# First attention: one ones-column product per unit on a VectorE sum, for units of three and four key blocks

## The reference

```python
qg = q.reshape(b, HKV, G, s, D)
scores = jnp.einsum('bkgqd,bkpd->bkgqp', qg, k) * scale
scores = jnp.where(causal, scores, jnp.float32(-1e+30))
probs = jax.nn.softmax(scores, axis=-1)
out = jnp.einsum('bkgqp,bkpd->bkgqd', probs, v).reshape(b, H, s, D)
```

## Time and profile before

| what | value |
|---|---|
| runs | 1920.54, 1912.13, 1920.51 us |
| median | 1920.51 us |
| span of the profiled execution | 1921.2 us, 0.7 us above the median |
| TensorE busy | 1731.9 us, 90% |
| VectorE busy | 1151.9 us, 60% |
| ScalarE, GpSimd busy | 708.0 us (37%), 784.0 us (41%) |
| granted TensorE clock, mean | 0.980 of full speed; 1.00 in the stretches up to 800 us |
| last column maxima of a 3-block unit of the first attention | at 770.3 us |
| window 130 to 770 us | TensorE 613.39, VectorE 439.00, GpSimd 347.89, ScalarE 254.90 of 640 us |

### The profile page before, as it was taken

How to read it: one execution, slowest core, us unless ns; L and a number is a source line. 1 busy time by engine, 2 the same in 40 slices (tenths; PEclk the granted TensorE clock), 3 DMA queues, 4 the chain that set the end, 5 groups by cost and what they waited for, 6 DMA issues and landing times.

```text
span 1921.2 us, 76644 instructions
## 1 busy us (share of the span) xinstructions
PE 1731.9 (90%) x34928; PEld 1286.5 (67%) x34928; DVE 1151.9 (60%) x2281; ACT 708.0 (37%) x1073; POOL 784.0 (41%) x760
## 2 busy tenths in 40 slices
PE   6899999999999999798999989899899898878993
PEld 4667777777777767564562767677676676668883
DVE  4656666666787875667337655666666566544324
ACT  2333444344334333342430333343333343334341
POOL 2555646564646463324250403325232343015442
PEclk9999999999999999998999999999999999989997
DMA  9600000000000000300021123131321313025666
GB/s 306 203 2 2 2 2 2 2 2 2 2 2 2 2 2 2 111 1 1 1 67 19 40 61 77 40 87 46 84 73 43 85 44 84 20 66 179 205 205 185
DMA packets 81043, 113.48 MB, mean 59 GB/s; under 512 B 9485, under 2 KB 63505, under 8 KB 80288
## 3 DMA queue, kind: packets, MB, share of 16 engines
q1 hardware_dynamic: 71376, 97.16, 18.6%
q0 software_dynamic: 4544, 8.54, 1.3%
q10 hardware_dynamic: 4800, 2.89, 0.6%
HBM read 83.25 MB, written 45.68 MB: 67 GB/s over the span
## 4 chain that ended last, share of the span: by engine, by line
PE 66%; DVE 18%; issue 5%; ACT 4%; DMA 4%; POOL 2%; POOLq 0%; ACTq 0%; SPq 0%; DVEq 0%
PE psum L1189 63%; DVE colmax L1935 3%; DMA arena<-in_pack 3%; ACT prob L1664 3%; DVE colmax L2092 2%; DVE ctx_sum L1947 2%; DVE raw L1923 1%; DVE rowmax L1942 1%; PE psum L1544 1%; DVE arena L2028 1%; DVE rowmax L2100 1%; PE psum L1256 1%; ACT arena L1681 1%; PE psum L1264 1%; DVE prob L1987 1%
## 5 line engine op out<-in xcount | busy, mean ns | idle before, releaser
L1189 PE MATMUL psum<-arena 128*32 128x32 f32 (+8 forms) x10552 | 576.8, 247 | 43.9 <-issue 17.2
L1189 PEld LDWEIGHTS psum<-arena 128*32 128x32 f32 (+4 forms) x10552 | 453.5, 124 | 135.1 <-issue 61.0
L1681 ACT ACTIVATE arena<-psum 128x1024 f32<-128x1024 f32 (+1 forms) x192 | 169.4, 882 | 339.8 <-PE psum L1189 339.8
L1189 PE MATMUL psum<-neg_ident,rowmax 128*32 128x128 bf16 (+3 forms) x4352 | 208.2, 248 | 10.1 <-issue 8.4
L1935 DVE TENSOR_REDUCE colmax<-psum 128x512 bf16<-128x2048 f32 (+2 forms) x96 | 168.3, 1753 | 79.4 <-PE psum L1189 79.4
L2092 DVE TENSOR_REDUCE colmax<-psum 128x256 bf16<-128x768 f32 (+2 forms) x160 | 178.2, 1114 | 59.7 <-PE psum L1189 57.3
L1189 PE MATMUL psum<-prob,ffw 128*32 128x128 f32 x5120 | 201.5, 275 | 10.9 <-DVE rowmax L1942 9.6
L1696 ACT COPY ctx_sum<-psum 128x384 f32<-128x384 f32 x128 | 61.4, 479 | 378.4 <-PE psum L1189 330.8
L2330 POOL TENSOR_TENSOR arena<-ctx_sum 128x256 f32<-128x256 f32 x128 | 94.7, 740 | 228.5 <-DVE ctx_sum L1947 216.9
L2100 DVE TENSOR_REDUCE rowmax<-psum 128x2 bf16<-128x256 f32 (+1 forms) x192 | 97.9, 510 | 145.8 <-PE psum L1189 145.7
L1664 ACT ACTIVATE prob<-psum 128x2048 f32<-128x2048 f32 (+3 forms) x128 | 158.6, 1239 | 26.3 <-PE psum L1189 25.8
(11 more groups left out here) (270 smaller groups left out, 2532.1 us busy)
## 6 DMA issues: line engine op xcount, KB each, us to landing
arena<-in_pack SPq DMA_DIRECT2D x39, 578.0 KB, 3.9
sent<-in_empty SPq DMA_DIRECT2D x9, 2112.0 KB, 35.9
arena<-qk_parts SPq DMA_DIRECT2D x96, 128.0 KB
q_copies<-arena SPq DMA_DIRECT2D x32, 256.0 KB, 3.9
prob<-q_copies SPq DMA_DIRECT2D x128, 64.0 KB, 3.5
qk_parts<-arena SPq DMA_DIRECT2D x16, 384.0 KB, 3.7
arena<-sent SPq DMA_DIRECT2D x39, 132.0 KB, 3.3
ffw<-in_L_w SPq DMA_DIRECT2D x1, 2048.0 KB, 9.3
```

Of the source, the lines that this page charges most:

```text
L1189: return pe.matmul(o, lhsT, rhs, start=start, stop=stop, skip_group_check=True)
L1681: act.activation(probs_of(i)[:, :, h0 * P:(h0 + nh) * P], slot(n)[:, 0:(i + 1) * W].rearrange("p (j c) -> p j c", c=W), ACT.Exp, scale=HD1 ...
```

## The change

For units with `i >= SUMMED` = 2, those of three and four key blocks, a new step `sums` is put between `between` and `scores` of n + 2. On VectorE it waits for `exp` of n, and for the `values` that last read `prob_sum`, and adds the key blocks of `prob` into `prob_sum` (128 x 512, f32, in SBUF, one buffer). In `values` of such a unit the loop over the key blocks has only the two groups of `v0`; behind it TensorE waits for `summed` and multiplies `ones_col` by `prob_sum`, once per head. Units of one and two key blocks are as before.

```diff
+SUMMED = 2
...
+        prob_sum = sb("prob_sum", [P, BANK])
...
-        units = []
+        units, summed_of = [], {}
...
                 for f in between.get(n, []):
                     f()
+                if u["i"] >= SUMMED:
+                    summed_of[n] = add("sums", u=u)
                 if n + 2 < len(st):
                     scores(st[n + 2])
...
                         for j in range(i + 1):
-                            for c in range(3):
+                            for c in range(3 if n not in summed_of else 2):
                                 for h in range(GRP):
...
+                        if n in summed_of:
+                            w.wait_ge(summed, summed_of[n].n + 1)
+                            for h in range(GRP):
+                                ins = mm(psum[QUAD * h:QUAD * (h + 1), CTX, 2 * P:CW], ones_col[:, :],
+                                         prob_sum[:, h * P:(h + 1) * P], False)
                         ins.then_inc(ctx_full, 1)
...
+                    elif k == "sums":
+                        u = s["u"]
+                        n = u["n"]
+                        w.wait_ge(prob_ready, n + 1)
+                        w.wait_ge(ctx_full, max([m for m in summed_of if m < n], default=-1) + 1)
+                        dve.tensor_reduce(prob_sum[:, :].rearrange("p (z c) -> p z c", z=2),
+                                          prob_of(u).rearrange("p z j c -> p z c j"), AX.X, ALU.add).then_inc(summed, 1)
```

More of the change, by code:

```diff
@@ L1038, in build @@
                                    "prob_ready", "ctx_full", "ctx_drained", "recip"))
+        summed = semaphore("summed")
         colmax_ready = {"v": colmax_dve, "a": colmax_act}
```

## The result

The changed kernel takes 2015.72 us (median of 4 runs, 2012.87 to 2017.83) against 1919.51 us of the kernel before in the same comparison: ratio 1.0506, interval 1.0479 to 1.0533, **5.1% slower**, +96 us. The prediction had the sign and said +15. The profiled execution took 2012.87 us, its span is 2011.1 us, 89.9 us more than that of before.

What follows compares the result with a forecast made beforehand. It took a loop of waits through TensorE, VectorE and ScalarE in the first attention as the bound. Seven batches +4.8, first batch +1.8 and slot choice +8.5 made +15.1 us on the 1920.51 median: 1936 us, range 1917 to 1954.

Steps and rivals of the forecast that it cites:

- the price of the sum of four blocks: VectorE's sum of a four-block unit: 2.29 us, taken from column maxima in PSUM, 2.22 us held with overlap.
- The 3-block sum: VectorE's sum of a three-block unit: 1.76 us, taken from column maxima in PSUM, 1.69 us held with overlap.
- A: Four-block unit of a quarter; its sum, ahead of the column maxima of C, would cost 3.64 us a batch.
- C: Three-block unit of a quarter; its sum, ahead of the next quarter's first column maxima, would cost 1.44 us a batch.
- The first batch: First attention, where VectorE also makes `rope_a` in two quarters: 6.24 us late less 4.40 saved, +1.8 us.
- the choice of slots: VectorE's extra work in batches 5 to 7, ahead of four-block column maxima: +8.5 us over seven quarters.
- a collision with GpSimd: Rival: GpSimd's use of SBUF stretches VectorE's sums by 1.66, adding 74 us, 2010 us in all; chance 4%.
- nothing for GpSimd: GpSimd's work behind delayed VectorE maxima was taken as 0, since the chain doesn't pass through GpSimd there.
- the saving: TensorE's `values` lose five groups of `ones_col` a quarter, 0.22 us each: 1.10 us a quarter, 35.2 us in all.
- the third quarter: Third quarter of a batch: VectorE's 1.27 us wait for TensorE swallows the 1.10 us delay, leaving 0.
- TensorE's new waits: 64 waits on `summed` ahead of ones groups, taken as 0; rival: 0.2 us each, 1949 us, chance 9%.
- The rule behind the sign: On VectorE, idle time ahead of column maxima hides a sum; only the excess makes the maxima late, +15.1 us net.

Runs made afterwards that it cites:

- g1: The changed kernel, but its four-block reduction adds groups of four neighbouring elements, giving meaningless sums; 1953.84 us, ratio 1.0186 to the kernel before.
- e1: The changed kernel without the sums, the one ones product left reading block 0 of `prob`; 1894.95 us, ratio 0.9871 to the kernel before.
- g2: The changed kernel with sums one block smaller and moved just ahead of their own `values`, run again in a later session; 1903.94 us, ratio 0.9933.
- e2: The kernel before plus the sums, which nobody reads, every ones product left as before; 2036.7 us, ratio 1.0609 to the kernel before.
- f4: The changed kernel with the last block left out of each sum and the sums moved just ahead of their own `values`; 1980.33 us, ratio 0.9941.
- f2: The changed kernel with each sum moved behind the row maxima of the next unit but one, ahead of its own `values`; 2043.0 us, ratio 1.0254.
- f3: The changed kernel with the last block left out of each sum and given its own ones product, place unchanged; 2011.64 us, ratio 1.0097.
- e4: The changed kernel with only the three-block units summed on VectorE; 1936.86 us, ratio 1.0080 to the kernel before.
- e3: The changed kernel with only the four-block units summed on VectorE; 1999.25 us, ratio 1.0414 to the kernel before.

## Why the prediction was wrong, and where it was right

**The step that failed most: the price of the sum of four blocks.** It was taken from column maxima in PSUM, with the words "a source in another memory that is read at the same pace can win no more than that". The pace was assumed and not shown; it was the one thing that the rows couldn't show. It is 3.73 us, not 2.29, and it is the order of reading in that memory that costs. The 3-block sum is 1.90, not 1.76. With 3.66 and 1.83 us held, and the prediction's own idle times: A delays by 2.50 + 3.06 + (2.54 - 1.27) + (2.56 - 0.16) = 9.23 us a batch, C by 1.58, less 4.40 makes +6.4; seven of them 44.9. The first batch has 2 x (3.48 + 1.22) + 2 x 0.86 - 4.40 = 6.7, the choice of slots 5 x 1.16 + 2 x 1.83 = 9.5. The sum is **+61 us** instead of +15. On the chip the price of the 4-block sum alone is worth more than these 46 us: between g1 and the change lie 60.

The range had no such value because both of its bounds on the price came from the same rows. The stretch by 1.66 from rows 9 gave 3.7 us for this sum and 2010 us for the kernel, nearly the measured time, but by a collision with GpSimd, and as a rival of 4%. That mechanism is not the one: the sums take 3.67 to 3.80 us wherever they stand, the neighbours' form in the same place 2.27, and the 3-block sums do not stretch to 2.8. The Trainium skill (SBUF — State Buffer, "Who interferes with whom") has reductions free of such collisions, and these runs agree. The Trainium skill's formula for the fixed cost (VectorE: DVE Perf Modes, the section on the TRN2 errata) gave an estimate of 2.19 us; the trace agrees for neighbours (2.27) and is far from it for four separate places (3.73), where the measurement decides.

**The second step: nothing for GpSimd ("I take 0").** Of the 35 us left, some 20 are missed in g1 too (36 measured, 17 by the same sum with 1.90 for three blocks), with sums of about the price that was taken. In e1 some 11 us of the saving don't arrive even without any sum, and its chain then goes through GpSimd ahead of the shuffle; g1 shows the same wait delaying centering, sum and maxima in the fourth quarter. That this is GpSimd's doing is read from the traces; no run with a shorter rotation tests it. The prediction asked only whether the chain of before went through GpSimd. It should have asked what would be the last to arrive once TensorE's part is 1.1 us shorter. By the changed kernel's own trace this is worth some 15 us, an estimate: batch 2, whose fourth quarter kept the full clock, is 8.5 us longer, where the sum with the measured prices has 6.4, so 2.1 us a batch are missed, seven times.

**The third: no term for the clock.** Before, the granted clock was 1.00 in the stretches up to 800 us. Over the whole execution the mean was 0.980 before and is 0.959 in the changed kernel, 0.970 in g1 and 0.983 in g2. Within the first attention it was 1.00 before, 0.95 in the changed kernel and 0.97 in g1. Windows of the changed kernel, two of 150 us and two fourth quarters (busy time of matmuls, weight loads, VectorE, ScalarE and GpSimd, then the granted clock, DMA share and GB/s), against the first of them before:

```profile
300.00:450.00 150.00, 129.57 (x1821) 91.88 (x1822) 119.30 (x154) 55.16 (x79) 77.99 (x74) 0.98 0.01 2
450.00:600.00 150.00, 130.24 (x1760) 92.82 (x1760) 120.44 (x161) 51.92 (x73) 71.51 (x69) 0.92 0.01 2
329.05:356.61 27.56, 22.11 (x322) 15.74 (x320) 22.43 (x38) 9.81 (x16) 13.24 (x13) 1.00 0.00 1
536.77:567.14 30.37, 24.87 (x322) 17.42 (x320) 22.80 (x39) 9.80 (x16) 13.23 (x13) 0.89 0.01 1
```

```profile
300.00:450.00 150.00, 145.07 (x2308) 107.49 (x2307) 100.46 (x170) 60.70 (x87) 88.56 (x86) 1.00 0.01 2
```

The last two rows of the first fence are the same fourth quarter of two batches, with the same 322 matmul records: 27.56 us at clock 1.00, 30.37 at 0.89. VectorE has nearly the same work in both. TensorE in the first of them, then in the second:

```profile
344.65 0.40 PE L1194 MATMUL psum<-ident_bf,colmax 128*128 128x128 bf16 x4 [2.75 <-DVE colmax L1945]
344.97 1.14 PE L1194 MATMUL psum<-ffw 64*128 64x256 f32 x8
...
552.63 0.61 PE L1194 MATMUL psum<-ident_bf,colmax 128*128 128x128 bf16 x4 [3.02 <-DVE colmax L1945]
553.17 2.08 PE L1194 MATMUL psum<-ffw 64*128 64x256 f32 x8
```

In the first an idle of 2.75 us and the eight score matmuls in 1.14 us; in the second 3.02 us of idling, and behind it the same eight in 2.08 us, at 1.2 GHz. So a long wait can cost a second time. It doesn't always: TensorE's wait in the second quarters, here in batch 2, has such a fall too, and the 64 value matmuls behind it take 3.35 us instead of 1.96:

```profile
281.35 0.40 PE L1194 MATMUL psum<-ident_bf,colmax 128*128 128x128 bf16 x4 [3.00 <-DVE colmax L1945]
...
282.85 3.35 PE L1194 MATMUL psum<-prob,ffw 128*32 128x128 f32 x64
```

Yet the second quarters with it are no more than 0.3 us longer (24.93 to 25.14 us at 0.93 in batches 2 to 4, 24.82 at 1.00 in batch 6, which has the choice of slots besides): the column maxima behind them are held up by VectorE's own work. Between 130 and 863 us the changed kernel has 21 idle times of TensorE of 2.0 us and more. Behind 16 of them the clock is lower for a few us, the shortest of these being 2.03 us; behind five it isn't, one of them 3.02 us long. The batches of the changed kernel that I measured (from one fourth quarter to the next) are 102 to 107 us long, at clocks of 0.98 to 0.94; those of before 93 to 95. How much of the 96 us is clock can't be read exactly. The fourth quarters of batches 1 to 5 are 1.1, 0, 2.6, 2.8 and 1.0 us longer than the 27.56 us of the one at full clock, 7.5 us together, an estimate. Batches 3 and 4, with fourth quarters at 0.89, are 2.8 and 3.7 us longer against before than batch 2. These, the batches with the choice of slots, and the last one hold the some 20 us that are left of the 35 once 15 are put down to GpSimd. g1's fourth quarters fell to 0.88 and 0.94 as well, so the some 20 us that g1 misses hold clock too. No run separates the two.

**Right** were these. The saving is at its place: `values` of a 4-block unit shorter by three groups, 1280 records less. The sums are exposed where they were said to be, and the third quarter swallows most of its delay (0.1 us shorter, where 1.1 was said). TensorE's new waits cost nothing of their own: e2 without any has the loss, f4 with all 64 is faster than before. The rule behind the sign, idle time against the length of the sum, also held: f2 and f3 came within some 5 us of what it gave, e4 8 us above its 1929 us and inside the 1940 that were allowed for the clock. e3 lies 6 us above what was allowed.

**Open** is why the step lies between three and four places; no run varies anything that would tell it. The exact shares of GpSimd and the clock are open too, and whether another order of VectorE's list (shuffle behind the row maxima) would give g2 the rest of its 21 us; it wasn't tried.

## What to carry to other kernels

A duration borrowed from another memory is no price until the same access pattern has been seen from that memory: here a VectorE reduction of f32 that gathers from four or more separate places in SBUF costs 1.8 ns per element against 1.2 for three, so leave one block out rather than pay for it. Put a side computation next to the work of its consumer, not between two links of the chain: the same sums cost +96 us ahead of the column maxima and +49 ahead of their own `values`, and there, with one block fewer, they pay. When you shorten one engine's part of a loop, look for the wait that comes second there (GpSimd's here), and look at the granted clock behind a wait of TensorE: here it fell behind most idle times of 2 to 3 us, and cost next to nothing where VectorE was the last to arrive anyway.

## What the runs showed of the hardware that was not expected

- A VectorE reduction of f32 in SBUF: 2.27 us for 2048 elements in groups of neighbours, 3.60 to 3.79 us in groups from four places 16 B to 2 KB apart, 3.78 from eight. With three places 1.90 us for 1536 elements, with four 2.84. From PSUM, with four places 1 KB apart, 2.28 us.
- TensorE's granted clock fell to its lower level inside a busy loop, behind 16 of the 21 idle times of 2.0 us and more in the changed kernel (130 to 863 us), also behind one of 2.03 us, but not behind one of 3.02. Eight score matmuls take 1.95 to 2.08 us there instead of 1.14.
- A wait that has been met, ahead of matmuls that keep the tile size, adds nothing to the 0.21 us between two groups.
